# A three-layer graph attention stack with feed-forward on one Trainium2 core: the neighbour scores go through DRAM instead of TensorE, and every engine's order is written anew

## The reference

```python
h = relu(layernorm(x))                       # input normalisation
for l in range(3):
    si = h @ attn_w[l, :256]; sj = h @ attn_w[l, 256:]
    scores = leaky(si[:, :, None] + sj[:, None, :] + attn_b[l], 0.2)
    attn = softmax(where(mask, scores, -inf))
    y1 = h + attn @ h
    z = layernorm(y1, g1[l], beta1[l])
    ff = gelu(z @ W1[l] + b1[l]) @ W2[l] + b2[l]     # 256 -> 1024 -> 256
    h = layernorm(z + ff, g2[l], beta2[l])
out = x + h
```

## Time and profile before

| what | value |
|---|---|
| median of 3 runs | 1359.9 us (1359.55 to 1360.2) |
| profiled execution | 1360.92 us, span 1359.1 us from the first to the last instruction |
| busy in the span | PE 1267.5, PEld 1133.0, DVE 1128.7, ACT 924.8, POOL 658.0 us |
| mean granted TensorE clock | 0.987 of full |

### The profile page before, as it was taken

How to read it: one execution, slowest core, us unless ns; L and a number is a source line. 1 busy time by engine, 2 the same in 40 slices (tenths; PEclk the granted TensorE clock), 3 DMA queues, 4 the chain that set the end, 5 groups by cost and what they waited for, 6 DMA issues and landing times.

```text
span 1359.1 us, 23270 instructions
## 1 busy us (share of the span) xinstructions
PE 1267.5 (93%) x8065; PEld 1133.0 (83%) x8065; DVE 1128.7 (83%) x3325; ACT 924.8 (68%) x1754; POOL 658.0 (48%) x538
## 2 busy tenths in 40 slices
PE   0599999999999999999999999999999999999994
PEld 0388888888888898988888898998888898989983
DVE  4778788889997888889898878879998888888773
ACT  3476766677776677677777776777777677677751
POOL 1235434553565355345545543553565445445454
PEclk9699999999999999999999999999999999999997
DMA  6100001001221000001121100000121100000012
GB/s 205 62 17 17 16 32 40 0 1 41 69 61 50 1 1 1 1 1 32 55 63 32 40 1 1 1 1 3 58 80 41 32 1 1 1 1 1 1 32 78
DMA packets 39265, 39.91 MB, mean 29 GB/s; under 512 B 1736, under 2 KB 37612, under 8 KB 39148
## 3 DMA queue, kind: packets, MB, share of 16 engines
q1 hardware_dynamic: 39148, 38.43, 8.9%
HBM read 30.04 MB, written 8.39 MB: 28 GB/s over the span
## 4 chain that ended last, share of the span: by engine, by line
PE 59%; DVE 26%; POOL 7%; issue 4%; DMA 2%; ACT 1%; SPq 0%; POOLq 0%; DVEq 0%
PE acc L700 28%; PE hbank L685 23%; DVE xs L536 7%; POOL rstd L332 3%; PE util L735 3%; DVE hid_lo L435 3%; PE acc L715 3%; DVE st L454 3%; DVE xs L523 2%; PE util L742 2%; DVE mv L415 2%; DVE st L422 1%; DMA hb<-in_x_dram 1%; DVE st L530 1%; POOL xout L375 1%
## 5 line engine op out<-in xcount | busy, mean ns | idle before, releaser
L700 PE MATMUL acc<-w2hi,hid_hi 128*128 128x256 f32 x1536 | 441.4, 287 | 0.0
L700 PE MATMUL acc<-w2hi,hid_lo 128*128 128x256 f32 x1536 | 434.3, 283 | 0.0
L700 PE MATMUL acc<-w2lo,hid_hi 128*128 128x256 f32 x1536 | 434.1, 283 | 0.0
L332 POOL TENSOR_TENSOR rstd<-ve,halfs 128x4 f32<-128x4 f32 x112 | 122.7, 1095 | 598.2 <-DVE ve L417 598.0
L595 ACT ACTIVATE hbank<-hbank,vec 128x512 f32<-128x512 f32 x384 | 254.6, 663 | 188.2 <-PE hbank L685 184.9
L685 PE MATMUL hbank<-ht_hi,w1hi 128*128 128x512 f32 x768 | 320.2, 417 | 2.5 <-DVE hid_lo L435 2.5
L685 PE MATMUL hbank<-ht_lo,w1hi 128*128 128x512 f32 x768 | 302.6, 394 | 0.0
L685 PE MATMUL hbank<-ht_hi,w1lo 128*128 128x512 f32 x768 | 301.2, 392 | 0.0
L435 DVE TENSOR_TENSOR hid_lo<-hbank,hid_hi 128x512 fp32r<-128x512 f32 x384 | 258.8, 684 | 46.3 <-ACT hid_hi L601 46.3
L700 PEld LDWEIGHTS acc<-w2lo,hid_hi 128*128 128x128 f32 x1536 | 293.7, 191 | 4.0
L700 PEld LDWEIGHTS acc<-w2hi,hid_hi 128*128 128x128 f32 x1536 | 293.3, 191 | 4.0
(11 more groups left out here) (62 smaller groups left out, 1750.1 us busy)
## 6 DMA issues: line engine op xcount, KB each, us to landing
xres<-in_x_dram SPq DMA_DIRECT2D x16, 512.0 KB, 4.0
out_dram<-xout SPq DMA_DIRECT2D x32, 256.0 KB, 2.3
xraw<-in_x_dram SPq DMA_DIRECT2D x14, 512.0 KB, 3.7
xout<-in_L_gnn_W_dram SPq DMA_DIRECT2D x12, 512.0 KB, 3.9
adji<-in_adj_dram SPq DMA_DIRECT2D x16, 256.0 KB, 2.9
hb<-in_x_dram SPq DMA_DIRECT2D x2, 512.0 KB, 9.6
attn_rows<-in_L_gnn_attn_w_dram SPq DMA_DIRECT2D x1, 768.0 KB, 5.7
ln_rows<-in_L_gnn_g_dram SPq DMA_DIRECT2D x2, 384.0 KB, 7.4
```

The lines of the kernel that those rows point to most:

```text
L332: pool.tensor_tensor(rstd[n][:], ve[n][:], halfs[:], ALU.pow).then_inc(rstd_n[n], 1)
L700: mm = pe.matmul(to, v[:, k % HID, of_g], w[:, i.l, c], start=c == 0 and n == 0 and g % HG == 0, stop=c == C - 1 and n == 2, skip_group_ch ...
```

## The change

Four things change together. The row of sj no longer passes through PE and `util`: SP sends `dots[:, 1]` (128 partitions x 4 numbers) to a DRAM scratch (`send_sj`) and loads it back, repeated over all partitions (`load_sj`), into the new tile `sj_bc`; `masked` reads that tile, with a stride of four numbers, where it read PSUM. The orders of all engines are written anew. The first four weight halves have a staging buffer each (two in `xout`, one in `xs`, one in `xres`), and the loads of the opening are issued in a written-out list with no waits. `diag` is bfloat16. The diff, cut to its core; where a `slot` is redrawn only the new order stands, the old one is in the code above:

```diff
+        sj_bc = sb("sj_bc", [P, P, GG])
+        sj_dram = nc.dram_tensor("sj_dram", [2, P, GG], F32).ap()
...
-        diag = sb("diag", [P, P])
+        diag = sb("diag", [P, P], BF16)
...
-        b2_rows = xres[:, 0:L]
+        b2_rows = xs[:, 1, 0:L]
...
-        def half_staged(n, w):
-            t = xout[:, n % 2]
-            return t.rearrange("p g d -> p (g d)") if w == 0 else t
+        def half_staged(n):
+            t = (xout[:, 0], xout[:, 1], xs[:, 2], xres[:])[n if n < 4 else n % 2]
+            return t if halves[n][1] else t.rearrange("p g d -> p (g d)")
+        def half_arrived(n):
+            return (w_in[n], 16) if n < 4 else (w_in[n % 2], 16 * (n // 2))
...
+                if n >= 4:
+                    sp.wait_ge(w_lo, n - 1 if n >= 6 else n - 3)
+                sp.dma_start(half_staged(n), half_in_dram(l, w, h)).then_inc(half_arrived(n)[0], 16)
+            def send_sj(i):
+                sp.wait_ge(dotj_n, i.q + 1)
+                wait(sp, sj_in, 16 * (i.q - 1))
+                sp.dma_start(sj_dram[i.q % 2], dots[:, 1]).then_inc(sj_sent, 16)
+            def load_sj(i):
+                sp.wait_ge(sj_sent, 16 * (i.q + 1))
+                wait(sp, mask_n, i.q)
+                sp.dma_start(sj_bc[:].rearrange("p j g -> p (j g)"),
+                             sj_dram[i.q % 2].rearrange("j g -> (j g)").partition_broadcast(P)).then_inc(sj_in, 16)
...
+                if 4 <= s + 5 < len(halves):
+                    load_weights(s + 5)
...
+                if d:
+                    send_sj(d)
+                    load_sj(d)
+            load_xraw(item(0))
+            load_small()
+            load_adj(item(0))
+            load_xraw(item(1))
+            load_b2_rows()
+            load_weights(0)
+            load_weights(1)
+            load_ln1_rows()
+            load_xraw(item(2))
+            load_weights(2)
+            load_weights(3)
+            load_ln2_rows()
+            for s in range(-6, ITEMS + 3):
...
+                o, t, f, b, d = item(s - 2), item(s - 1), item(s), item(s + 1), item(s + 3)
+                if o and o.l == L - 1:
+                    add_input(o, 0)
+                if o:
+                    x_beta(o, 1)
+                if d and d.l == 0:
+                    make_rstd("0", d.g)
+                if o and o.l == L - 1:
+                    add_input(o, 1)
                 if t:
                     make_rstd("2", t.q)
+                if f:
+                    h_beta(f, 0)
+                if t:
                     x_gamma(t, 0)
+                if f:
+                    h_beta(f, 1)
+                if b:
+                    make_rstd("1", b.q)
+                    h_gamma(b, 0)
+                if t:
+                    x_beta(t, 0)
+                    x_gamma(t, 1)
                 if b:
                     h_gamma(b, 1)
                 if s == -3:
                     pool.wait_ge(ln1_in, 16 * 3)
                     pool.tensor_tensor(ln1_rows[:, 1], ln1_rows[:, 1], b2_rows, ALU.add).then_inc(ln1_ready, 1)
...
-                dve.wait_ge(sj_n, i.q + 1)
                 wait(dve, et_n, i.q)
-                dve.tensor_tensor(sc[:], pen[:, i.g % PENS], util[:].rearrange("p (g j) -> p g j", g=GG),
+                dve.wait_ge(sj_in, 16 * (i.q + 1))
+                dve.tensor_tensor(sc[:], pen[:, i.g % PENS], sj_bc[:].rearrange("p j g -> p g j"),
...
+                t, f, b, a, d, p = item(s - 1), item(s), item(s + 1), item(s + 2), item(s + 3), item(s + 4)
                 if s == -3:
                     dve.wait_ge(vec_turned, 1)
                     dve.tensor_copy(vec[:], util[:, 0:NV]).then_inc(vec_ready, 1)
+                if t:
+                    residual(t, 1)
+                if a:
+                    i_dots(a)
+                    add_bias(a)
+                if f:
+                    low(f, 0)
+                if t:
+                    moments2(t)
+                if f:
+                    low(f, 1)
+                if b:
+                    attend(b, 0)
+                    attend(b, 1)
+                if t:
+                    norm2(t, 0)
                 if f:
                     low(f, 2)
+                if b:
+                    moments1(b)
+                if f:
                     low(f, 3)
+                if d and d.l == 0:
+                    penalty(d)
+                if t:
+                    norm2(t, 1)
+                if a:
+                    masked(a)
+                if b:
+                    norm1(b)
+                if f:
+                    low(f, 4)
+                if p and p.l == 0:
+                    input_moments(p)
+                if b:
+                    h_low(b, 0)
+                if f:
+                    low(f, 5)
+                    low(f, 6)
+                    low(f, 7)
+                if a:
+                    minus_max(a)
+                if b:
+                    h_low(b, 1)
                 if d:
+                    j_dots(d)
+                if p and p.l == 0:
+                    input_shift(p)
                 if f:
                     residual(f, 0)
+                split_weights(s + 4)
+            for s in range(-6, ITEMS + 3):
                 slot(s)
...
+                if i.q == 1:
+                    act.wait_ge(ln1_ready, 1)
+                if i.q == 2:
+                    act.wait_ge(w_lo, 3)
...
+                t, f, b, d = item(s - 1), item(s), item(s + 1), item(s + 3)
+                if b:
+                    leaky(b)
+                if t:
+                    gelu_high(t, 7)
+                if f:
+                    h_high(f, 1)
+                if b:
+                    exps(b)
+                if f:
+                    gelu_high(f, 0)
+                if b:
+                    et_out(b)
+                if f:
+                    gelu_high(f, 1)
+                if d and d.l == 0:
+                    first_x(d)
+                if f:
+                    gelu_high(f, 2)
+                round_weights(s + 4)
                 if f:
                     gelu_high(f, 3)
                     gelu_high(f, 4)
+                    gelu_high(f, 5)
+                    gelu_high(f, 6)
+                if b:
+                    h_high(b, 0)
+            for s in range(-6, ITEMS + 3):
                 slot(s)
...
-            def sj_rows(i):
-                    mm = pe.transpose(util[:, g * P:(g + 1) * P], dots[:, 1, g:g + 1].to_broadcast([P, P]), ident[:])
-                mm.then_inc(sj_n, 1)
...
-                    pe.wait_ge(mask_n, i.q + 2)
+                    pe.wait_ge(eto_n, i.q + 1)
...
+                f, b, a = item(s), item(s + 1), item(s + 2)
+                if f:
                     ffn2(f, 6)
+                    ffn2(f, 7)
+                if b:
+                    ffn1(b, 0)
+                    ffn1(b, 1)
+                if a:
+                    e_turn(a)
+                if b:
+                    ffn1(b, 2)
                 if a:
                     aggregate(a, 0)
                     aggregate(a, 1)
+                if b:
+                    ffn2(b, 0)
+                    ffn1(b, 3)
+                    ffn2(b, 1)
+                    ffn1(b, 4)
+                    ffn2(b, 2)
+                    ffn1(b, 5)
+                    ffn1(b, 6)
+                    ffn2(b, 3)
+                if a:
+                    z1_turn(a, 0)
+                if b:
+                    ffn1(b, 7)
+                    ffn2(b, 4)
+                if a:
+                    z1_turn(a, 1)
+                if b:
+                    ffn2(b, 5)
+            for s in range(-6, ITEMS + 3):
                 slot(s)
```

160 lines of the change are left out of this document (24 added, 136 removed).

## The result

The changed kernel takes 1303.8 us (median of 4 runs, 1303.67 to 1305.02) against 1359.8 before. The ratio is 0.959, with a 95% interval from 0.957 to 0.961: 56 us faster. The profiled execution took 1305.02, of which its span is 1303.2. I had forecast 1306, with a range from 1300 to 1315.

The account below looks back on a forecast made before the run. PE, busy 1267.5 of 1359.1 us, was taken as the bound, with 31.4 us of waits, mainly for norm1. Start 54.5, stretch 1235.1 and tail 15.5 gave a 1305.1 span, forecast 1306, range 1300 to 1315.

Parts of the forecast that it names:

- start, stretch and tail: Span split at the first ffn1 and the last residual: 54.5, 1235.1 and 15.5 us forecast.
- the rival that I said it took in: DVE stays the bound: POOL meetings keep the twelve input items at 27.73 us, total 1326; chance 0.17.
- The transposes: Leaving PE, they save 0.44 us each; 46 in the stretch give 20.2 us, full items take 25.64.
- my terms for it: Opening of the stretch: 4.2 us off for work done ahead, 2.3 for slow opening matmuls, 0.4 for item 1's e_turn.
- norm1 and the 31.4 us of waits: On DVE, norm1 unhindered by POOL takes 2.33 us, not 3.39 to 4.12; PE's 31.4 us of waits go.
- The first round: Items with split_weights paid 1.4 us extra for low behind the split; moved ahead of moments2, nothing left.
- The input items: Twelve items with a coming group's input statistics keep 0.4 us each, 5 in all; bounds 0 and 25 us.
- The trip: Two DMAs per item carry the row through DRAM in 6.5 us, hidden in 13.7 between j_dots and masked.
- the slower rival: DRAM trip exceeds 13.7 us; each us beyond costs 48 us, 1368 at a 15 us trip; chance 0.05.
- The start: Loads issued at once, but item 0 waits for the row; first ffn1 at 54.5, 3.3 us off, bounds 52 and 58.
- The lock as a rival: Shared-port lock lets POOL hold DVE at j_dots or masked, up to 1.8 us per item; total 1326, chance 0.17.
- one of my own signs of being wrong: In the changed kernel's trace, j_dots stretching beside POOL's add_input would show the forecast wrong.

Follow-up runs that it names:

- run 2: The changed kernel with the sj row made by PE's transposes again, all other new orders kept: 1313.1 us, ratio 0.966.
- run 4: The kernel before with only POOL's first h_gamma moved directly behind make_rstd 1: 1342.6 us, ratio 0.988.
- run 3: The changed kernel with POOL's x_beta and x_gamma put back ahead of the first h_gamma: 1339.4 us, ratio 0.985.
- run 10: The changed kernel with one more POOL wait, so add_input of the second half starts only when j_dots is done: 1300.1 us, ratio 0.957.
- run 5: The changed kernel with scratch and sj_bc laid out group by group, so masked reads its row contiguously: 1322.0 us, ratio 0.972.
- run 1: The kernel before with only the sj row sent through DRAM and PE's transposes gone, old orders kept: 1421.4 us, ratio 1.045.
- run 8: The changed kernel with three DRAM-to-DRAM copies of the row between write and load: 1313.3 us, ratio 0.966.

## Why the prediction was right, step by step

**The place of the limit was right.** I divided the run into start, stretch and tail, and each came out within 2.1 us: 54.5 said and 52.4 measured, 1235.1 and 1235.3, 15.5 and 15.5. The forecast was 1306, the median is 1303.8; the start makes the difference. That the middle came within 0.2 is partly luck, as the next steps show. The ends of my range were not those that I had worked out (1298.5 below, and above 1326, the rival that I said it took in).

**The transposes: 0.44 us each.** Ordinary items fell by 0.50, to 25.58, where I had 25.64. Against run 2, in the same orders, they differ by exactly 0.44. The 0.06 left is not the order of PE's calls, since run 4 keeps the old one and its ordinary items take 26.01: it came with the place of POOL's instructions. So 26.08 was not quite PE's own time, as I had read it, although the window shows PE busy for all of it. Over 48 items 0.06 is 2.9 us. The opening of the stretch took as much more than my terms for it (minus 4.2, plus 2.3, plus 0.4), and these two misses cancel: 48 x 25.58 + 6.1 is 1233.9, and 1.4 remain for the opening, for which I had minus 1.5. That is luck.

**norm1 and the 31.4 us of waits.** I said 2.33 and no wait; it is 2.35 and none outside the start. The middle's gain without the trip is 31.5 in run 2, of which the 0.06 of each item are about 3. That `norm1` meeting POOL was the cause is shown from both sides by runs 3 and 4. What I did not see is how sharp it is: the path fits by 1.6 us, and a growth of 2.0 is over that.

**The first round.** Costed at nothing left, and nothing is left: 25.58. But I had laid its whole 1.4 us to `low` behind the split. Run 4, which moves POOL alone, takes these items from 27.50 to 26.6, so 0.9 of it was the wait for `norm1`.

**The input items.** I had 0.4 us for each of twelve, 5 in all. It is 6.1 over ten. The cause I named, `j_dots` near `add_input`, is one part (run 10: 3.5 of the 6.1). What I had missed is `masked` at 1.09 for 0.68 and `ve` at 1.3 for 0.17, both ahead of `h_low`. Run 2, with `masked` at 0.68 and PE 0.44 slower, shows no excess; how much of the other 2.6 each of them makes is not shown, since in run 5 late trips hide it. The trace of before had no strided read of this kind; run 5 shows the stride as the cause of `masked`'s longer time. The Trainium skill (SBUF — State Buffer, section "Door 1: The DMA port swizzle (why `[64,N]` ≈ `[32,N]`)") says that SBUF is read in lines of 16 bytes and that each access that moves to another line pays. In `sj_bc` every number of `masked` is 16 bytes behind the last, and by that rule the trace agrees, 1.09 against 0.69.

**The trip.** I took 6.5 us and 13.7 of room; it is 5.5 of 12.9 in ordinary items (13.9 in the first round). The mechanism of the slower rival is right (runs 1, 5, 8), but its price was too high: I had 48 us for each us beyond the limit. In run 5 `masked` waited 23.7 us in mid-run and the items grew by 10, since a late `masked` has the 1.6 us of `norm1`'s path before PE waits, and since 26 of the 45 later items waited, not all.

**The start.** I had the first weight half at 14.3 and the row at 28 to 30. The half came at 16.6, 2.3 later; the row at 30.6. Yet the first `ffn1` came 2.1 earlier than said: laid end to end, my durations from the row to it were 24.5 to 26.5 us, and they are 21.8. That chain was over-costed, and I did not separate which piece of it; which step there was too dear stays open.

**The lock as a rival.** I gave 0.17 to the case that DVE stays the bound by meetings with POOL. The meetings came, in the input items alone, and `j_dots` beside `add_input` was one of my own signs of being wrong; they cost 6.1 us in all at most, not 20. The Trainium skill (SBUF — State Buffer, section "SBUF: two separate sides") has VectorE and GpSimd exclude each other where a VectorE instruction reads two inputs from SBUF and GpSimd's reads SBUF too; the trace agrees for `j_dots`, 1.49 beside POOL and 0.42 alone, and run 3 for `masked`, 2.17 and 1.09. What kept it small is the place: in ordinary items POOL is idle there.

## What to carry to other kernels

An edit that takes work off the busiest engine and the order around it are two changes: here the edit alone cost 62 us, the order alone gave 47, and both together 56. Price a round trip not by its length but by the distance, in the queue of the engine that waits, between the instruction that starts it and the one that needs it; and give the first item, for which there is no such distance, the old way. When one engine's queue is full to the last half microsecond, look first for where it meets an instruction of POOL, since the place of one or two such instructions moved 4 to 36 us.
